# A routed two-layer kernel: mixed rows kept in place, routing one-hots of 64 rows by 16 columns, and the first two up steps in pieces of 128 slots

## What is computed

```python
out = jnp.einsum('bct,bcd->bdt', x, weights[subjects])   # 32 x 32 mixing of each sample
flat_x = out.reshape(N, Dq)                              # 4096 mixed rows of 256
logits = flat_x @ Wg + bg                                # 4 experts, the best 2 of each token
for i in range(E):                                       # capacity 1024 slots per expert
    score = jnp.where(assigned, probs[:, i], -jnp.inf)
    sel_p, sel_idx = jax.lax.top_k(score, capacity)
    h = gelu(flat_x[sel_idx] @ W1[i])
    y = h @ W2[i] * p
    out = out.at[sel_idx].add(y)
x = x + out                                              # layer 0, then layer 1:
x = x + ((silu(gate) * up) @ Wd ...) @ w.T + bias        # each with low-rank adapters by sample
```

## Time and profile before

| | |
|---|---|
| median of three runs | 633.85 us (632.81 to 633.86) |
| the profiled execution | 633.1 us, span 631.3 us |
| mean granted clock | 0.974 |
| TensorE busy | 589.1 us, 93% |
| VectorE busy | 365.2 us, 58% |
| ScalarE busy | 248.5 us, 39% |
| GpSimd busy | 130.6 us, 21% |

### The profile page before, as it was taken

The page is one execution under the profiler, slowest core; times in us unless marked ns, Lnnn a source line. Parts: engine busy times, 40 slices in busy tenths (PEclk is TensorE's granted clock), DMA queues, the critical chain, the costliest instruction groups (busy, mean ns, idle before and its releaser), DMA issues.

```text
span 631.3 us, 9585 instructions
## 1 busy us (share of the span) xinstructions
PE 589.1 (93%) x3240; PEld 488.9 (77%) x3240; DVE 365.2 (58%) x790; ACT 248.5 (39%) x548; POOL 130.6 (21%) x112
## 2 busy tenths in 40 slices
PE   4736789999999999999999999999999999999994
PEld 2623579999999999987888888888888888888883
DVE  6838876876687556665445554454455454544533
ACT  2615235764874764655233413322333133223110
POOL 3000140644444442654002002020030030000000
PEclk9969779999999999999999999999999999999998
DMA  8993729416319312552004104022041040120012
GB/s 315 322 347 113 254 66 394 72 41 179 52 37 328 54 43 27 111 140 67 2 1 122 21 0 131 13 88 54 2 120 21 0 129 12 65 43 4 12 22 33
DMA packets 63931, 60.88 MB, mean 96 GB/s; under 512 B 37328, under 2 KB 56272, under 8 KB 62544
## 3 DMA queue, kind: packets, MB, share of 16 engines
q1 hardware_dynamic: 52880, 37.99, 19.8%
q0 software_dynamic: 8832, 22.09, 14.3%
q10 hardware_dynamic: 2176, 0.26, 0.3%
HBM read 45.05 MB, written 19.47 MB: 102 GB/s over the span
## 4 chain that ended last, share of the span: by engine, by line
PE 85%; DMA 5%; DVE 4%; SPq 2%; issue 1%; ACT 1%; POOL 0%; DVEq 0%; ACTq 0%; POOLq 0%
PE bank L1157 24%; PE bank L1158 23%; PE bank L1159 23%; PE bank L1391 5%; PE bank L1358 2%; PE bank L1356 2%; DMA xT<-in_xT 2%; DMA flat_rows<-flat_st 1%; DMA x_sb<-in_x 1%; SPq L370 1%; DVE passed L823 1%; PE bank L1267 1%; DVE onehot_r L874 1%; PE bank L1350 1%; PE bank L1365 1%
## 5 line engine op out<-in xcount | busy, mean ns | idle before, releaser
L666 ACT ACTIVATE act<-bank 128x512 f32<-128x512 f32 x64 | 38.3, 598 | 187.4 <-PE bank L1391 187.4
L1114 DVE TENSOR_TENSOR prod<-bank,act 128x512 f32<-128x512 f32 x64 | 44.2, 690 | 115.6 <-PE bank L1391 114.3
L1016 DVE TENSOR_TENSOR hid_lo<-hf,hid_hi 128x512 fp32r<-128x512 f32 (+1 forms) x72 | 45.5, 633 | 48.2 <-ACT hf L602 43.9
L1159 PE MATMUL bank<-w_hi,hid_lo 128*128 128x256 f32 x256 | 72.5, 283 | 0.0
L1157 PE MATMUL bank<-w_hi,hid_hi 128*128 128x256 f32 x256 | 72.2, 282 | 0.3 <-DVE hid_lo L1016 0.3
L1158 PE MATMUL bank<-w_lo,hid_hi 128*128 128x256 f32 x256 | 72.3, 282 | 0.0
L599 ACT ACTIVATE hid_hi<-bank 128x512 fp32r<-128x512 f32 (+1 forms) x72 | 39.7, 552 | 67.4 <-PE bank L1159 62.5
L448 POOL DMA_INDIRECT x_rows<-y_sb,slot_row x32 | 52.9, 1654 | 45.6 <-ACT y_sb L568 35.4
L437 POOL DMA_INDIRECT xg<-flat_rows,slot_row x32 | 33.2, 1037 | 136.6 <-DVE slot_row L883 88.7
L468 POOL DMA_INDIRECT b_pair<-b_rows,b_row x8 | 8.7, 1083 | 223.0 <-PE bank L1410 222.4
L1157 PE MATMUL bank<-xs_hi,w_hi 128*128 128x512 f32 (+1 forms) x142 | 54.0, 380 | 0.0
(11 more groups left out here) (279 smaller groups left out, 1284.9 us busy)
## 6 DMA issues: line engine op xcount, KB each, us to landing
w_raw<-in_L_ffn_W SPq DMA_DIRECT2D x8, 1024.0 KB
flat_rows<-flat_st SPq DMA_DIRECT2D x8, 520.0 KB, 7.0
xT<-in_xT SPq DMA_DIRECT2D x8, 512.0 KB, 8.4
x_sb<-in_x SPq DMA_DIRECT2D x8, 512.0 KB, 8.7
outT<-out_sb SPq DMA_DIRECT2D x120, 32.0 KB
b_rows<-b_all_hi SPq DMA_DIRECT2D x1, 1152.0 KB
b_rows<-b_all_lo SPq DMA_DIRECT2D x1, 1152.0 KB
wdT<-in_wdT SPq DMA_DIRECT2D x1, 1024.0 KB, 5.6
```

What stands on the lines that cost most here:

```text
L666: act.activation(act1[h % 2][:, :], bank[h % 2][:, :], ACT.Silu).then_inc(silu1, 1)
L1016: dve.tensor_tensor(lo[:, n], hf[s % 2][:, n], hi[:, n].bitcast(f32), ALU.subtract).then_inc(hid0, 1)
L1114: dve.tensor_tensor(prod[h % 2][:, :], bank[2 + h % 2][:, :], act1[h % 2][:, :], ALU.mult).then_inc(prod1, 1)
L1159: return pe.matmul(out, ll, rh, start=False, stop=stop, skip_group_check=True)
```

## The change

Three things, and what they need.

1. `x_sb` gets rows of 260 values. ScalarE writes the mixed rows and the probabilities over the x rows there, the staging tiles and their waits go, and one semaphore counts the stores.
2. The slot's place is split as 64 rows and 16 blocks, so `onehot_r` has 64 columns and `onehot_q` 16. Two values per token stand in `slotted` (the group number counts from 1, so that a sum of 0 tells an empty slot). `route` has two products for each group, on the two halves of the array's columns.
3. The first two up steps are cut into four pieces of 128 slots, each run when its gather has come. W1 of the first expert is loaded before the fold weights, its high parts are made after items 19 and 21, its low parts in search steps 5 to 8, in halves of a row; W2 is loaded after the fourth store, and its low pieces are made between the slots' low parts. Two filler products stand before the second gather, and no others after the first eight.

The diff, cut to its core:

```diff
-        x_sb = sb("x_sb", [P, G, D], f32)
+        x_sb = sb("x_sb", [P, G, ROWP], f32)
...
-        flat_st = [sb(f"flat_st{i}", [P, GB, ROWP], f32) for i in range(4)]
...
+        FIRST_BANKS = (6, 7, 4, 5)
+        LO_STEPS = (4, 5, 6, 7)
+        LO_W1, LO_ALL = len(LO_STEPS), len(LO_STEPS) + 2
...
+            load_w1(0)
+            sp.wait_ge(x_in[7], 16)
             for dst, src in ((wfT, A["wfT"]), (wdT, A["wdT"]), (bdT, A["bdT"])):
                 sp.dma_start(dst[:, :, :], src.rearrange("(k p) n -> p k n", p=P)).then_inc(fold_w_in, 16)
-            sp.wait_ge(x_in[7], 16)
-            load_expert(0, raw0_in)
...
-                sp.dma_start(flat_v[:, i * GB:(i + 1) * GB, :], flat_st[i % 4][:, :, :]).then_inc(flat_out[i % 4], 16)
+                sp.dma_start(flat_v[:, i * GB:(i + 1) * GB, :], x_sb[:, i * GB:(i + 1) * GB, :]).then_inc(flat_out, 16)
+                if i == ROWS_FIRST // GB - 1:
+                    sp.wait_ge(raw0_in, 16)
+                    load_w2(0)
...
-                    if n >= 4 * GB and n % GB == 0:
-                        act.wait_ge(flat_out[n // GB % 4], 16 * (n // GB // 4))
-                    last = act.activation(flat_st[n // GB % 4][:, n % GB, 0:D], src[:, 0:D], ACT.Copy)
+                    last = act.activation(x_sb[:, n, 0:D], src[:, 0:D], ACT.Copy)
...
+                if n in (ROWS_FIRST + 3, ROWS_FIRST + 5):
+                    k = (n - ROWS_FIRST - 3) // 2
+                    if k == 0:
+                        act.wait_ge(raw0_in, 16)
+                    act.activation(w1[0][:, k, :], w1_raw[:, k, :], ACT.Copy).then_inc(hi0, 1)
...
+                if i in LO_STEPS:
+                    k, at_ = LO_STEPS.index(i) // 2, LO_STEPS.index(i) % 2 * HID // 2
+                    dve.wait_ge(hi0, k + 1)
+                    dve.tensor_tensor(w1[1][:, k, at_:at_ + HID // 2], w1_raw[:, k, at_:at_ + HID // 2],
+                                      w1[0][:, k, at_:at_ + HID // 2].bitcast(f32), ALU.subtract).then_inc(lo0, 1)
...
-                link(dve.tensor_tensor(onehot_q[:, g, :], over(pos_q[:, e, g], Q),
-                                       iota_b[:, 0:Q].unsqueeze(1).to_broadcast([P, n, Q]), ALU.is_equal))
+                i = done(dve.tensor_tensor(onehot_q[:, g, :], over(pos_q[:, e, g], Q2),
+                                           iota_b[:, 0:Q2].unsqueeze(1).to_broadcast([P, n, Q2]), ALU.is_equal))
+                dve.tensor_tensor(onehot_r[:, g, :], over(pos_r[:, e, g], R2),
+                                  iota_b[:, 0:R2].unsqueeze(1).to_broadcast([P, n, R2]), ALU.is_equal)
+                dve.wait_ge(chain, i)
                 dve.tensor_tensor(slotted[:, g, :, :], over(onehot_q[:, g, :], C),
-                                  vals[:, g, :].unsqueeze(2).to_broadcast([P, n, Q, C]), ALU.mult)
-                dve.tensor_tensor(onehot_r[:, g, :], over(pos_r[:, e, g], P),
-                                  iota_b[:, :].unsqueeze(1).to_broadcast([P, n, P]), ALU.is_equal).then_inc(route_in, 1)
+                                  vals[:, g, :].unsqueeze(2).to_broadcast([P, n, Q2, C]), ALU.mult).then_inc(route_in, 1)
...
+            for c in range(GB):
+                if c < 2:
+                    first_w2_lo(c)
+                first_lo(c)
...
-                    last = pe.matmul(bank[7][:, 0:Q * C], onehot_r[:, g, :], slotted[:, g, :, :].rearrange("p q c -> p (q c)"),
-                                     start=g == 0, stop=g == G - 1)
+                    for j in range(2):
+                        last = pe.matmul(bank[7][j * R2:(j + 1) * R2, 0:Q * C], onehot_r[:, g, :],
+                                         slotted[:, g, j * Q:(j + 1) * Q, :].rearrange("p q c -> p (q c)"),
+                                         start=g == 0, stop=g == G - 1, tile_position=(0, j * R2))
...
+            def first_up(c):
+
+                pe.wait_ge(xs_hi, c + 1)
+                pe.wait_ge(xs_lo, c + 1)
+                cs = slice(c * P, (c + 1) * P)
+                for h in range(2):
+                    for k in range(KD):
+                        last = product(bank[h][:, cs], at(w1, every, k, slice(h * P, (h + 1) * P)), at(xs[0], every, k, cs),
+                                       start=k == 0, stop=k == KD - 1)
+                    if c == GB - 1:
+                        last.then_inc(up0, 1)
+
+            first_transposed(0)
+            keep_busy(WAIT_ROWS, bank[2], w1)
+            first_transposed(1)
+            pe.wait_ge(lo0, LO_W1)
+            for c in range(2, GB):
+                first_up(c - 2)
+                first_transposed(c)
+            for c in range(2, GB):
+                first_up(c)
...
-                if s == 0:
-                    first_up()
-                else:
+                if s >= 2:
```

More of the change, by code:

```diff
@@ L16 @@
 NAD = 8
-C = 3
+C = 2
 SB = BT // 32
@@ L268, in adaln_moe_lora @@
         fold_w_in, raw0_in, raw1_in = sem("fold_w_in"), sem("raw0_in"), sem("raw1_in")
-        flat_out = [sem(f"flat_out{i}") for i in range(4)]
+        flat_out = sem("flat_out")
         x1_init, spare_out = sem("x1_init"), sem("spare_out")
@@ L402, in _ @@
                     sp.wait_ge(w2_new, KH * (e - 1))
-                load_expert(e, raw0_in)
+                load_w1(e)
+                load_w2(e)
                 if e == 1:
@@ L427, in _ @@
             pool.memset(mix[:, :, :], 0.0).then_inc(zeroed, 1)
-            pool.memset(vals[:, :, 2], 1.0).then_inc(vals_in, 1)
             def gather(b):
@@ L451, in scatter @@
                         in_=y_sb[half][:, q, :], in_offset=None, compute_op=ALU.add).then_inc(scattered, 16)
-            for i in range(4):
-                pool.wait_ge(flat_out[i], 32)
+            pool.wait_ge(flat_out, 128)
             pool.wait_ge(spare_out, 32)
@@ L590, in adapter_column @@
                 return act.activation(a_pair[par][:, KD:, 3, r], a_all[1][:, 2 * KD:, bass.ds(at_, RANK)].bitcast(f32), ACT.Copy)
-            for k in range(KD):
-                slots_hi(0, k, bank[6 + k])
+            for c in range(GB):
+                first_hi(c)
+            slot_scales(0)
             for s in range(STEPS0):
@@ L888, in _, with first_lo, first_w2_lo @@
             route_read(0)
+            def first_lo(c):
+                dve.wait_ge(xs_hi, c + 1)
+                hi, lo = (t[:, :, c * P:(c + 1) * P] for t in xs[0])
+                dve.tensor_tensor(lo, bank[FIRST_BANKS[c]][:, 0:KD * P].rearrange("p (k n) -> p k n", k=KD), hi.bitcast(f32),
+                                  ALU.subtract).then_inc(xs_lo, 1)
+            def first_w2_lo(i):
+                a = pieces(w2_raw)[i]
+                dve.wait_ge(hi0, KD + i + 1)
+                dve.tensor_tensor(w2[1][:, a, :], w2_raw[:, a, :], w2[0][:, a, :].bitcast(f32), ALU.subtract).then_inc(lo0, 1)
             def slots_lo(b, k, src):
-                dve.wait_ge(xs_hi, KD * b + k + 1)
+                dve.wait_ge(xs_hi, parts_before(b) + k + 1)
                 hi, lo = xs[b % 2]
@@ L1003, in _ @@
             places(slice(1, E))
-            n = 0
-            for r, (hi, lo) in ((w1_raw, w1), (w2_raw, w2)):
-                for a in pieces(r):
-                    n += 1
-                    dve.wait_ge(hi0, n)
-                    dve.tensor_tensor(lo[:, a, :], r[:, a, :], hi[:, a, :].bitcast(f32), ALU.subtract).then_inc(lo0, 1)
-            for k in range(KD):
-                slots_lo(0, k, bank[6 + k])
+            for c in range(GB):
+                if c < 2:
+                    first_w2_lo(c)
+                first_lo(c)
             for s in range(STEPS0):
@@ L1206, in item @@
                         pe.wait_ge(x_in[n // GB], 16)
-                    last = pe.matmul(out[:, 0:D], mix[:, n, :], x_sb[:, n, :], start=True, stop=True)
+                    last = pe.matmul(out[:, 0:D], mix[:, n, :], x_sb[:, n, 0:D], start=True, stop=True)
                 elif n < ITEMS - 1:
@@ L1271, in _, with first_transposed @@
             pe.wait_ge(ident_in, 1)
-            pe.wait_ge(hi0, 4)
+            pe.wait_ge(hi0, KD)
             pe.wait_ge(item_ev, ITEMS)
             keep_busy(WAIT_GATHER, bank[2], w1)
-            for k in range(KD):
-                slots_transposed(0, k, bank[6 + k])
-            keep_busy(WAIT_PARTS0, bank[2], w1)
-            pe.wait_ge(lo0, 4)
+            def first_transposed(c):
+                pe.wait_ge(gathered[c], 16)
+                for k in range(KD):
+                    last = pe.transpose(bank[FIRST_BANKS[c]][:, k * P:(k + 1) * P].bitcast(f32r),
+                                        xg[:, c, k * P:(k + 1) * P].bitcast(f32r), ident_r[:, :])
+                last.then_inc(xsT, 1)
+            def first_up(c):
[3 more added lines that the diff above has]
+                for h in range(2):
+                    for k in range(KD):
+                        last = product(bank[h][:, cs], at(w1, every, k, slice(h * P, (h + 1) * P)), at(xs[0], every, k, cs),
[11 more added lines that the diff above has]
```

(14 more changed lines are left out.)

70 lines of the change are left out of this document (38 added, 32 removed).

## The result

| | before | after |
|---|---|---|
| median of four runs | 633.86 us (632.81 to 634.38) | 628.41 us (627.03 to 628.73) |
| ratio | | 0.9913, 95% interval 0.9892 to 0.9933 |
| profiled execution | 633.1, span 631.3 | 627.03, span 625.2 |
| mean granted clock | 0.974 | 0.972 |

The forecast was 627.5 us (622.5 to 632.0). The total is within 1 us of it. Its terms are not: the part up to batch 1 was forecast 9.9 us shorter (-6.0 without the 3.9 for the routes) and became 3.0 us shorter; the rest was forecast 3.9 us longer and became 3.1 us shorter.

A forecast was written before the change was run, and what follows sets the result against it. TensorE was taken to set 85% of the end, gapless from about 86 us, with the change working in the front before. Terms summed to -6.0 on the profiled 633.1, 627.1, or 627.8 as median; 627.5 given, range 622.5 to 632.

The forecast's parts named there:

- No staging tiles: Search in the front: ScalarE's copy no longer waits for a store, so the count reads lose their hole; -8.2 us.
- Splitting W1: Search steps: VectorE's four added subtractions cost 0.06 us in three steps and 0.6 in the seventh; +0.8 us.
- the rival with a wait for W1: Search: W1 lands late, ScalarE waits for it and the -8.2 shrinks to 0; 635.3 us, chance 0.05.
- One-hots: VectorE before the first gather: four parts at 1.13 us instead of 1.67, -2.2, and one link less in route_read, -0.1.
- Routing products: 64 products instead of 32: +0.25 us for the first route's tail, +3.9 for three later routes at 28 ns per product.
- halves side by side: Routes: 64 products take the time of 32 plus switches, 1.0 instead of 3.9, pieces at full clock; 623.2 us, chance 0.20.
- The estimate of 53 ns: Routes: 64-column weight load priced from the skill's page, +2.9 us per route, making the sum 4.9 us higher.
- Pieces: First two up steps: early pieces run while gathers are in flight, so step 2 starts sooner; -0.9 us.
- The gathers' company: First gather: starting earlier, it meets the end of layer 1's weight loads; +0.2 us.
- Clock in the search: Search: while TensorE is at half clock, a step costs some 0.2 us more; +0.2 us (0 to 0.6).
- The slower rival: Routes: loads run one behind the other at 73 ns per product, three routes cost 12.6 us; 635.8 us, chance 0.08.

The follow-up runs named there:

- e1: Kernel before with only the first part of the change (mixed rows over x, no staging tiles): 627.18 us, ratio 0.989.
- e9: Kernel before with only the tiles from xg on moved 416 bytes up, where the changed kernel has them: 627.97 us, ratio 0.9937.
- e5: Changed kernel with 40 unread products of five shapes in place of the eight fillers and 40 more in mid layer 0: one execution, 626.7 us.
- e4: Changed kernel with the old one-hots (128 rows, 8 columns, three values) and 32 whole-array routing products: 631.98 us, ratio 0.9984.
- e10: Changed kernel, 128-slot pieces kept, with small products in the search and more fillers up to step 2 to hold TensorE's clock: 619.34 us, ratio 0.9805.
- e11: e8 with more fillers in the first route, before the first gather and between gathers; first two up steps whole: 619.59 us, ratio 0.9818.
- e7: Changed kernel with only the tiles from xg on moved 32 bytes higher: 628.13 us, ratio 0.9924.
- e2: Changed kernel with the first two up steps whole, all 512 slots behind all transposes, fillers between them: 621.83 us, ratio 0.9804.
- e3: Changed kernel with the first two up steps in two pieces of 256 slots: 622.71 us, ratio 0.9827.
- e8: e2 plus four short unread products behind the items of search steps 3 to 8: 620.56 us, ratio 0.98.

## Why the prediction was right, and where it was not

1. **No staging tiles, -8.2: right.** The wait is gone, and e1 puts the part at -7.8 up to the gather.
2. **Splitting W1, +0.8: right.** Steps 5 to 8 of 2.77, 2.77, 3.37 and 2.77 us against 2.71, 2.71, 2.77 and 2.71 are +0.78. ScalarE's first piece of W1 begins at 33.79 us with no wait before it, so the rival with a wait for W1 falls.
3. **One-hots, -2.3: right.** 62.84 - 61.69 = 1.15 us a part, forecast 1.13.
4. **Routing products, +0.25 and +3.9: the mechanism right, the size not.** A product on a half of the array takes 17.5 ns, not 28; from the last down product to the next up product a route takes 1.32 us instead of 0.94, +0.38 and not +1.3. By the whole batches (e9) it is +0.62, so three make 1.9: nearest to the rival "halves side by side" (1.0), though no trace shows that two products ran at once. The estimate of 53 ns for a load of 64 columns, worked out from the page TensorE: Matmul & The Clock Gate (LDWEIGHTS) of the Trainium skill, is three times the 17.5 ns that these bf16 products show. For float32 products at full clock it fits: e5 has about 0.11 us for 128 columns, 107 ns by the page; at half clock they take 0.213, and the transposes 73 ns.
5. **Pieces, -0.9: wrong, +3.4, and +1.9 behind it.** The step that failed is the price of a product of 128 columns, "73 ns full, about 120 half", taken from the transposes in the earlier trace rows. Those have the same shape, and even load as many float32 weight columns, but an up product costs 0.111 us at full clock and 0.213 at half (after, e4, e5). 48 products of 128 columns cost 48 x 0.213 = 10.2 us where 12 of 512 cost 12 x 0.427 = 5.1. At full clock (e10 against e11) the cut costs 0.5 and gains nothing. I had given half clock to pieces 0 to 2 and let it end there; it lasted through step 2 and the first downs to 88.2 us. Behind the last gather's issue that is 15.7 us, 14.0 in e7 and 15.4 in e4, which have the pieces too, and 8.5 to 10.5 in e1, e2, e3 and e9, which have whole steps or halves. What returns it so late isn't settled. About 1.5 us of the 5.3 belong to the trace of the kernel before, whose clock was back early.
6. **The gathers' company, +0.2: 0.** From the first gather's issue to the transposes of its rows it is 2.99 us, 3.00 before, and from 68 to 70 us the DMA engines moved nothing.
7. **Clock in the search, +0.2: too small.** The early fall cost the same before and after (a wait of 0.65 in each). A second one was not foreseen: +0.2 in the ninth step, and the tenth, whose items are fold products of twice the work, pays 1.5 in the profiled execution (0.4 in e3; e8 takes it away).
8. **What had no term: the pace of the stream, about -5.** I took code that isn't touched to cost the same. The last stretch became 3.1 us shorter though the routes in it took 1.9 more. e9 shows that the moved tiles did it, and by its trace they were worth 6.0 there. Had I had the addresses in view, no row of the kernel before could have priced them.

The misses of items 5 and 7 (about +7.7), of item 4 and the first read (-2.8) and the pace (about -5) cancel. That the total came out within 1 us is luck. Without the moved tiles, which the forecast didn't know, it would have been 4 us or more slower by e9, at the range's upper end or beyond. The slower rival's price, 73 ns per routing product, was a factor of four off.

## What to carry to other kernels

Before a matrix product is cut into narrower ones, its price is to be taken from a row of the same operation with as many weight columns; a transpose of the same shape was the wrong row. Here a float32 piece of 256 streamed columns or fewer costs what one of 256 costs. In a front where TensorE mostly waits, filler products that keep its clock up were worth more (6.8 us) than the finer overlap they stood beside; taking the overlap out was worth as much, and the two didn't add up. And a change that moves tiles in memory is to be compared with the old kernel at the new addresses, or its gain may be put down to the wrong part: here 4 of the 5.5 us came with the addresses.

## What the hardware showed that I had not expected

- The same stream of float32 products ran at 45.68, 46.48, 46.56 or 46.80 us per two batches, by nothing but the place of its tiles (416, 32, 448 and 0 bytes up from where the kernel before has them). The down products of 256 columns account for most of it: 12 of them take 90.10 to 91.49 = 1.39 us after and 90.23 to 91.67 = 1.44 before, and there are 72 such groups in the kernel. The cause isn't settled.
- Products of 64 bf16 weight columns on two halves of the array, taking turns, were issued 17.5 ns apart, faster than whole-array products of 128 weight columns and 24 streamed ones (25 ns).
- A product with 128 float32 weight columns and up to 256 streamed ones costs 0.111 to 0.12 us at 2.4 GHz and 0.213 us at 1.2 GHz: it goes by the granted clock. A transpose with the same columns costs 73 ns and about 120.
- The clock's level in a gap differs between executions that do nearly the same there: at 70 to 72 us e7 was granted 0.99, the changed kernel, of the same program but for 32 bytes, 0.50.
